# A decoder layer in five stages: what lies ready when a stage begins, and in which order its first work stands

## The reference

```
xz = LN(x) @ W_in; conv of 4 taps, silu, x_dbl = xb @ W_x, dt = softplus(dt_low @ W_dt + b_dt)
h_t = h_(t-1) * exp(A * dt_t) + (x_t * dt_t) * B_t           (1024 channels x 16 states, 224 steps)
y_t = sum over the states of h_t * C_t;   x1 = x + ((y + xb * D) * silu(z)) @ W_out
q = LN(x1) @ Wq + bq (16 heads of 32);  k, v = context @ Wk + bk, context @ Wv + bv
x2 = x1 + softmax(q k^T / sqrt(32)) v @ Wo + bo
router: softmax(gelu(LN(x2) @ rW1 + rb1) @ rW2 + rb2), the two best of 4 experts for each row
out = x2 + sum over both experts e of weight_e * (gelu(LN(x2) @ We1[e] + be1[e]) @ We2[e] + be2[e])
```

## Time and profile before

| | us |
|---|---|
| median of three runs | 2700.24 |
| the profiled execution's own time | 2700.03 |
| its span, from the first to the last recorded instruction | 2698.2 |
| PE busy, share of the span | 2388.7, 89% |
| DVE busy | 1457.8, 54% |
| POOL busy | 1342.5, 50% |
| ACT busy | 1223.0, 45% |

### The profile page before, as it was taken

How to read it: one execution, slowest core, us unless ns; L and a number is a source line. 1 busy time by engine, 2 the same in 40 slices (tenths; PEclk the granted TensorE clock), 3 DMA queues, 4 the chain that set the end, 5 groups by cost and what they waited for, 6 DMA issues and landing times. The chain is left out here.

```text
span 2698.2 us, 39015 instructions
## 1 busy us (share of the span) xinstructions
PE 2388.7 (89%) x14144; PEld 1963.4 (73%) x14144; DVE 1457.8 (54%) x2039; ACT 1223.0 (45%) x2647; POOL 1342.5 (50%) x940
## 2 busy tenths in 40 slices
PE   7999499999999994789999999873989989998994
PEld 6866388888888872457666667652878878888883
DVE  7714599999999972355766676643112121121222
ACT  4345377777777640234444444433333333332331
POOL 2323477777777760266566656634360460009712
PEclk9999699999999996789999999885999999999997
DMA  4327956665666535455554555307130130002303
GB/s 113 131 72 225 273 173 199 203 193 175 194 198 201 161 106 152 125 129 119 132 130 121 140 119 127 94 21 247 47 118 31 48 124 23 16 31 92 118 31 117
DMA packets 236261, 341.90 MB, mean 127 GB/s; under 512 B 34594, under 2 KB 164578, under 8 KB 234962
## 3 DMA queue, kind: packets, MB, share of 16 engines
q1 hardware_dynamic: 213378, 280.03, 36.9%
q0 software_dynamic: 13728, 47.19, 5.6%
q10 hardware_dynamic: 9008, 12.78, 1.4%
HBM read 212.28 MB, written 127.65 MB: 126 GB/s over the span
## 5 line engine op out<-in xcount | busy, mean ns | idle before, releaser
L768 POOL TENSOR_TENSOR s_hc<-s_h,s_Cc 128x896 f32<-128x896 f32 x256 | 495.0, 1938 | 179.2 <-DVE s_h L882 94.9
L882 DVE TENSOR_TENSOR_SCAN s_h<-s_decay,s_ub 128x928 f32<-128x928 f32 x256 | 527.3, 2080 | 13.9 <-PE s_ub L909 7.1
L920 PE MATMUL s_yps<-s_hc,s_ident 128*128 128x224 f32 x2048 | 430.1, 353 | 1.1 <-POOL s_hc L768 1.1
L2000 DVE TENSOR_TENSOR e_hl<-e_ps,e_hh 128x256 fp32r<-128x256 f32 x256 | 108.7, 425 | 574.8 <-ACT e_ps L2040 574.8
L812 ACT ACTIVATE s_decay<-s_dt,s_A 128x224 f32<-128x224 f32 x1024 | 388.0, 470 | 20.2 <-DVE s_h L882 19.1
L920 PEld LDWEIGHTS s_yps<-s_hc,s_ident 128*128 128x128 f32 x2048 | 368.7, 191 | 1.9 <-POOL s_hc L768 1.4
L1219 DVE TENSOR_REDUCE t_nmax<-t_ps 112x1 fp32r<-112x752 f32 x256 | 240.2, 938 | 231.4 <-PE t_ps L1554 230.6
L1175 POOL TENSOR_TENSOR t_part<-t_pT 125x672 f32<-125x672 f32 x128 | 206.7, 1615 | 295.4 <-ACT t_pT L1465 292.5
L2059 PE MATMUL e_ps<-e_xTh,e_w1h 128*128 128x256 f32 x1024 | 292.9, 286 | 45.2 <-DVE e_xTl L1992 45.2
L2039 ACT ACTIVATE e_hh<-e_ps,e_b 128x256 fp32r<-128x256 f32 x256 | 121.6, 475 | 423.4 <-PE e_ps L2061 423.2
L1465 ACT ACTIVATE t_pT<-t_ps 125x448 f32<-125x448 f32 x384 | 181.3, 547 | 261.4 <-PE t_ps L1580 261.0
(11 more groups left out here) (221 smaller groups left out, 4360.9 us busy)
## 6 DMA issues: line engine op xcount, KB each, us to landing
s_ut<-ut_d SPq DMA_DIRECT2D x192, 128.0 KB, 3.3
e_stage<-in_L_ffn_We POOLq DMA_DIRECT2D x24, 1024.0 KB, 5.7
t_k<-kh_d SPq DMA_DIRECT2D x64, 375.0 KB, 6.4
xs_d<-s_zero SPq DMA_DIRECT2D x30, 512.0 KB, 3.5
ut_d<-a_x SPq DMA_DIRECT2D x32, 448.0 KB, 5.5
s_Cc<-cs_d SPq DMA_DIRECT2D x8, 1792.0 KB, 10.1
kh_d<-s_kh SPq DMA_DIRECT2D x32, 375.0 KB, 2.7
kl_d<-s_kl SPq DMA_DIRECT2D x32, 375.0 KB, 3.0
```

The costliest lines, as they stand in the source:

```text
L768: nc.gpsimd.tensor_tensor(hc[:, u % 2, k], h[:, u % 2, k, :, 2:SLOT], Cc[:, b % 2, k], ALU.mult).then_inc(hc_done, 1)
L882: nc.vector.tensor_tensor_scan(h[:, u % 2, k].rearrange("p n t -> p (n t)"), decay[:, u % 2, k].rearrange("p n t -> p (n t)"), ub[:, s % 2 ...
L920: ins = nc.tensor.matmul(yps[:, u % 2, 0:L], ident[:], hc[:, u % 2, :, n], start=(n == 0), stop=(n == NS - 1))
```

## The change

**A region of 36 KB in each partition, `carry`, outlives its stage.** In state_space it holds one of the two buffers of C, of the context and (as `even`, the same bytes in another type) of the matrices of B. In the last batch these are free, and SP loads there what the attention begins with: x and y of batch 0, Wq and W_out (`load_next_stage`, one piece a unit, five in all). In the last batch of scores of the attention (it = 7, sl 1 to 4) W_out, Wq, x and y are no longer needed, and SP loads the experts' first four chunks into the region (`load_first_weights`); in experts it is `stage`. The identity is loaded once for the kernel.

**Last sums.** The last unit's sums are taken by segment: 64 products of 56 columns, 16 as soon as a segment's products are there (`last_sums`), in the place of 16 of 224 columns.

**Attention's first transfers and queries.** Keys of the first two groups and y of batch 1 are loaded ahead of the first queries; the queries of batch 0 are computed in two banks in turn, stored, and loaded again by four heads as soon as they are stored (`load_first_queries`). The rows of the key tile are set by POOL, ahead of its other constants.

**Experts' first splits.** ACT makes the high parts of chunks 0 and 1, then the first tile's split, then chunks 2 to 5; POOL makes those of 6 and 7. DVE makes the low parts of 0 and 1, then the tile's, then 2 and 3, then the gates, then waits for b2.

```diff
@@ state_space, sync
+            def load_next_stage(i):
+                last = B - 1
+                if i == 0:
+                    sp.wait_ge(fill_done, NSEG * CC * last)
+                    sp.wait_ge(v_mm, NC * last)
+                    sp.wait_ge(hc_done, NSEG * CC * last)
+                    sp.dma_start(carry[0:TT, XT_AT:XT_AT + 2 * DM].rearrange("p (u d) -> p u d", u=2),
+                                 x[0].rearrange("(u p) d -> p u d", p=TT)).then_inc(carry_loaded, 16)
...
+                else:
+                    part = slice((i - 3) * 4, (i - 2) * 4)
+                    sp.dma_start(carry[:, WOUT_AT:WOUT_AT + CC * DM].rearrange("p (c n) -> p c n", n=DM)[:, part],
+                                 W_out.rearrange("(c p) n -> p c n", p=P)[:, part]).then_inc(carry_loaded, 16)
...
+                if b == B - 1 and 1 <= c <= 5:
+                    load_next_stage(c - 1)
@@ state_space, tensor
+            def last_sums(u):
+                for k in range(NSEG):
+                    pe.wait_ge(hc_done, NSEG * u + k + 1)
+                    if k == 0:
+                        pe.wait_ge(y_done, u - 1)
+                    for n in range(NS):
+                        ins = nc.tensor.matmul(yps[:, u % 2, k * SEG:(k + 1) * SEG], ident[:], hc[:, u % 2, k, n],
+                                               start=(n == 0), stop=(n == NS - 1))
+                ins.then_inc(sum_done, 1)
...
-            sums(UNITS - 1, range(NS))
+            last_sums(UNITS - 1)
@@ attention
-        wout, wq = sb("wout", [P, CC, DM]), sb("wq", [P, KC, DM])
+        wq = carry[:, 0:KC * DM].rearrange("p (k n) -> p k n", n=DM)
+        gT = carry[:, GT_AT:GT_AT + CC * L].rearrange("p (c t) -> p c t", t=L)
+        wout = carry[:, WOUT_AT:WOUT_AT + CC * DM].rearrange("p (c n) -> p c n", n=DM)
+        xt = carry[0:TT, XT_AT:XT_AT + 2 * DM].rearrange("p (u d) -> p u d", u=2)
...
+        def queries_bank(b, j):
+            return BANK5 if b == 0 and j % 2 == 1 else BANK6
@@ attention, sync
+            def load_first_queries(j):
+                sp.wait_ge(q_stored[j % 2], 32 * (j // 2 + 1))
+                for i, src in enumerate((0, 0, 1)):
+                    sp.dma_start(q3[i * DK:(i + 1) * DK, 0, 4 * j:4 * j + 4].bitcast(F32),
+                                 q_d[src, 0, j].rearrange("(r p) t -> p r t", p=DK)).then_inc(q_first[j], 16)
+            def load_first_weights(n):
+                g, second = n // 2, n % 2
+                if n == 0:
+                    sp.wait_ge(q_mm, KC * B)
+                    sp.wait_ge(out_mm, 2 * B)
+                    sp.wait_ge(x1b_done, 2 * B)
+                    sp.wait_ge(xn_done[0], 2 * B)
...
+                sp.dma_start(carry[:, n * KC * DM:(n + 1) * KC * DM].rearrange("p (k n) -> p k n", n=DM), src).then_inc(w_first[n], 16)
-            sp.dma_start(ident[:], ident_in).then_inc(first_loaded, 16)
-            load_g(0)
-            sp.dma_start(wout[:], rows(W_out)).then_inc(first_loaded, 16)
-            load_x(0)
...
+                if it == -1 and sl == 8:
+                    store_queries(0, 0)
+                    for j in range(KC):
+                        if j + 1 < KC:
+                            store_queries(0, j + 1)
+                        load_first_queries(j)
...
+                if it == B - 1 and 1 <= sl <= 4:
+                    load_first_weights(sl - 1)
@@ attention, gpsimd (and the same taken out of vector)
+            nc.gpsimd.memset(k3[ROWS3:ROWS3 + 2].bitcast(F32), 0.0).then_inc(rows_zeroed, 1)
+            pool.wait_ge(rows_zeroed, 1)
+            pool.wait_ge(w_loaded, 16 * N_W)
+            for r in range(4):
+                nc.gpsimd.tensor_scalar(k3[ROWS3:ROWS3 + 2, :, r], k3[ROWS3:ROWS3 + 2, :, r].bitcast(F32),
+                                        onehot[ROWS3:ROWS3 + 2, r % 2:r % 2 + 1], None, ALU.add).then_inc(rows_set, 1)
@@ attention, tensor
-            pe.wait_ge(first_loaded, 32)
...
-                else:
+                elif b >= 1:
                     pe.wait_ge(q_low, KC * b + j)
+                elif j >= 2:
+                    pe.wait_ge(q_low, j - 1)
@@ experts, gpsimd
-                if n >= 2 * WG:
+                if n >= 2 * WG - 2:
@@ experts, vector
+            for n in range(2):
+                low_weights(n)
...
+                def first(t):
+                    tokens(t)
+                    if e == 0:
+                        for n in range(2, 4):
+                            low_weights(n)
+                        gates()
+                        wait(dve, "b2_loaded", 16)
@@ experts, scalar
-            for n in range(2 * WG):
+            for n in range(2):
+                high_weights(n)
...
+                def first(t):
+                    tokens(t)
+                    if e == 0:
+                        for n in range(2, 2 * WG - 2):
+                            high_weights(n)
+                        wait(act, "b1_loaded", 16)
```

More of the change, by code:

```diff
@@ L910, in fill @@
                                            ut[:, u // 2 % 2, 2 * k + half, u % 2 * P:u % 2 * P + P],
-                                           diag[:, b % 2, 2 * k + half, first:end, 0:width], start=True, stop=True)
+                                           diag[b % 2][:, 2 * k + half, first:end, 0:width], start=True, stop=True)
                 ins.then_inc(fill_done, 1)
@@ new lines, in decoder @@
+        ident = sb("identity", [P, P])
+        mamba_in(nc, a["x"], a[s + "W_in"], a[s + "conv_w"], a[s + "conv_b"], a[s + "W_x"], a[s + "W_dt"], a[s + "b_dt"],
+                 a["identity"], ident, xb_d, z_d, dt_d, ut_d, bt_d, cs_d)
+        with nc.sbuf_tensor("s_even", [P, CARRY], F32R) as even:
+            pass
+        carry = sb("carry", [P, CARRY])
+        state_sems = state_space(nc, a[s + "A_log"], a[s + "D"], a["identity"], ident, even, carry, a["x"], a[s + "W_out"], a[t + "Wq"],
+                                 xb_d, z_d, dt_d, ut_d, bt_d, cs_d, y_d, a["ctxT"], a[t + "Wk"], a[t + "bk"], a[t + "Wv"],
+                                 kh_d, kl_d, v_d, xs_d)
```

225 lines of the change are left out of this document (114 added, 111 removed).

## The result

The changed kernel took 2674.19 us (median of four runs, 2671.8 to 2676.9), the kernel before 2699.67 us beside it: a ratio of 0.9908, 95% interval 0.9891 to 0.9925. Timed again later on another chip it took 2674.27 us, ratio 0.9885 (0.9866 to 0.9904). The forecast was 2673, its range 2657 to 2686. The profiled execution has a span of 2673.5 us, 24.7 less than before.

The account below looks back on a forecast made before the run. PE was taken to be near its limit in every stage, with dips at stage ends. Two shortened dips, at the attention's and experts' starts, gave 2700.0 - 16.3 - 11.0 = 2672.7 us; range 2657 to 2686.

Parts of the forecast that it names:

- Last sums: End of state_space: 128 passes paced by weight loads, 0.106 us each, 13.6 us; 6.2 us lost.
- Attention to the projection: Attention's start: PE waits for no transfer, 1.3 us allowed until it runs; projection keeps its 16.77 us.
- Key rows on POOL: Attention's start: POOL's additions, 4.6 us each, hold DVE's norm; costs 3.7 us (0 to 4.6).
- First queries: Attention, behind the norm: four query groups without waits between, 10.2 us, plus 1.0 for the last split.
- To x: Attention, values' start to landing of x of batch 1: values 14.7 us, then 15.2 us.
- Experts: Experts' start: first product 22.8 us earlier, second layer 13.5 earlier, 2.5 given back by the clock; 11.0 gained.
- E to end: From the experts' first instruction to the kernel's end: 11.0 us less.
- Moved transfers: Loads moved into the last batches of state_space and attention: cost nothing, 0 to 3 us each as bounds.
- X to E: From x of batch 1 landing (DVE's first add of it) to the experts' first instruction: no change forecast.
- Cheap passes: Rival: last unit's sums at 0.05 us a pass, POOL not holding the norm, b2 sooner; 2659 us, chance 0.17.
- late x: Rival: issuing the values takes SP as long as before, x lands at 1102.1; 2684 us, chance 0.19.
- the slower case: Rival: state_space's scan waits for small transfers behind new loads in its last batch; 2716 us, chance 0.03.

Follow-up runs that it names:

- Rows on DVE: Changed kernel with the key rows (a memset and four additions) made by DVE before its first step, not by POOL: 2672.34 us, ratio 0.9880.
- keys and y behind: Changed kernel with keys of the second group and y of batch 1 issued behind the first queries, not ahead: 2678.07 us, ratio 0.9901.
- Gates first: Changed kernel with DVE's six gate operations ahead of its first two low parts, wait for b2 left in place: 2671.31 us, ratio 0.9877.
- b2 at use: Changed kernel with gate operations ahead of the low parts and b2 waited for only where it is added: 2664.56 us, ratio 0.9843.
- region filled late: Changed kernel with the attention's first x, y, Wq and W_out issued behind state_space's whole SP loop, not inside its last batch: 2689.11 us, ratio 0.9941.
- weights in stage: Changed kernel with the experts' first four weight chunks issued by the experts' own SP program, not in the attention's last batch: 2681.44 us, ratio 0.9914.
- changed, again: The changed kernel run once more, nothing edited: 2674.27 us, ratio 0.9885 to the kernel before.
- x before values: Changed kernel with SP issuing x of batch 1 ahead of the values, not behind values, Wo, rows and router weights: 2654.02 us, ratio 0.9802.

## Why the prediction was right, step by step

**Last sums**: right in kind, small in size. Forecast 13.6 us at 0.106 a pass, measured 14.39 at 0.112; start of the stage 6.9 us later relative to POOL's last product, forecast 6.2. The load of 128 columns sets the pace. Scaled from the 31 loads of the earlier trace rows the bound was 0.115; that end was the nearer one.

**Attention to the projection**: PE began 0.04 us behind S (allowed: 1.3) and took 15.65 us instead of 16.77. Both helped, 2.4 us. But 1.1 of it is luck: in the second profile of the same kernel the projection took 16.52, and 15.5 to 16.9 in the others. In the first profile the granted clock was 0.66 in the projection's first 5 us, in the second 0.50.

**Key rows on POOL**: the four additions took 4.14 us each, not 4.6, and held the norm. Ten profiles have the rows on POOL. In six it was the small operation, 3.15 to 3.79 us as forecast (3.7). In four, the first profile among them, it came due before the fourth addition began and slipped in ahead, and the next operation was held instead, 1.8 to 2.1 us. Which of the two it was follows from the projection: due 17.4 to 17.7 us behind S it slipped in, due 18.0 or later it was held. *Rows on DVE* puts the hold at 3 us on the way to the queries' end.

**First queries**: forecast 10.2 + 1.0, measured 9.9 from the first product to the last low part's end. The values began 6.3 us behind that end, not 4.1: the last six loads alone took 4.0 us to issue. The values began at 1058.96 (forecast 1061.0).

**To x**: forecast 29.9 us from there, measured 29.7. It took 41.1 before, so this term holds 11.4 of the 26.0. That it held to 0.2 is partly luck: the values moved at 94 to 99 GB/s, not 104, and took until about 1074.5, 15.5 us for the 14.7; the rest took 14.2 for 15.2. Of the 11.4, *keys and y behind* gives back 5.0. The other 6 no run takes apart. The wait in DVE's third step was there, 23.65 us (forecast: some 20).

**Experts**: first product 9.4 us behind the start (forecast 9.6), second layer 26.4 (forecast 25.6). E to end gave 11.4, forecast 11.0. What the lower clock gives back was put at 2.5 from 5 us at half speed, which no row had shown; measured, the first six products and those behind them took 5.0 us, where they took 2.8 before, so it is 2.2. The last wait was named rightly in one only of the eight profiles with this experts' program, the second of the changed kernel. It should have been b2, with one of the gates' products held. In the first profile b2 was ready 24.2 us behind E, as worked out, yet both products were held, and the gates ended 1.3 us behind it. In the second b2 came last, though again behind two held products. *Gates first* shows b2 next, and *b2 at use* shows what stood behind both.

The prediction said that no row spoke for the second half of the SBUF rule. Its own had one: DVE's product of 64 elements, both inputs in SBUF, took 4.51 us and ended with POOL's low part. The changed kernel has more of them. POOL's low part that began while DVE's fourth low part was still running took 5.27 and 5.30 us, against 4.51 for the next one in the first run; and DVE's product of 64 elements ended with POOL's twice. The Trainium skill, page "SBUF — State Buffer", section "Who interferes with whom", lets a DVE operation with two SBUF inputs and a GpSimd operation that reads SBUF exclude each other, whoever comes first; these rows agree, in both directions. The second product even began 0.5 us before the low part that it waited out; POOL was issuing a transfer then, and what held the product in that half microsecond no run shows.

**Moved transfers**: nothing, as forecast; *region filled late* and *weights in stage* found no cost where they were taken away.

**What the sum did not have**: X to E grew by 5.2 us. PE's idle stretch before X is longer than it was, and its clock behind it would be the first suspect. Stretches behind X, PE's busy time (instructions), granted clock, DMA share, GB/s; before:

```profile
1107.17:1127.17 20.00, 14.04 (x54) 0.76 0.29 71
1127.17:1147.17 20.00, 18.79 (x135) 0.85 0.34 88
1147.17:1167.17 20.00, 13.53 (x103) 0.83 0.79 158
1167.17:1187.17 20.00, 19.15 (x117) 0.83 0.42 101
```

changed:

```profile
1088.70:1108.70 20.00, 15.34 (x49) 0.67 0.16 46
1108.70:1128.70 20.00, 18.43 (x129) 0.81 0.44 108
1128.70:1148.70 20.00, 14.12 (x105) 0.79 0.81 162
1148.70:1168.70 20.00, 18.33 (x109) 0.70 0.43 101
```

changed, again:

```profile
1089.32:1109.32 20.00, 13.69 (x53) 0.76 0.27 70
1109.32:1129.32 20.00, 19.13 (x135) 0.83 0.35 89
1129.32:1149.32 20.00, 13.20 (x97) 0.77 0.79 158
1149.32:1169.32 20.00, 19.15 (x117) 0.81 0.43 101
```

The first profile of the changed kernel reached the next batch's residual 84.1 us behind X, the kernel before 79.7, with PE busy for longer at a lower grant. But the length of the idle stretch does not decide it. PE had stood 22.3 us in the first profile and 24.7 in the second, and the second has nearly the grants of the kernel before and took 81.3. In *rows on DVE* PE had stood 24.1 us, the grants were 0.76 to 0.86, and it took 79.5. Nor does this stretch decide X to E, which was 739.9 in the second profile and 732.5 in *b2 at use*. So my theory of a longer stretch at the lower clock falls, and what divides the executions here is open. From the last residual to E the kernel before took 221.4 us, the thirteen profiles of the others 223.9 and more; with one profile of the kernel before, whether that is the change or chance stays open too. It was not tried apart.

The number is better than the sum behind it. x landed 2.2 us earlier than forecast, though S came 1.3 later; the experts gave 0.4 more; and X to E, which stood at nothing, took 5.2. That makes 2.6 too little in the profiled execution and 1.5 in the median, and that it is no more is luck. Cheap passes, late x and the slower case all fell: no 0.05 us pass, x issued 24.7 us behind the values, no wait for a transfer in the scan's last batch.

## What to carry to other kernels

At a stage's end, find the one transfer for which the pipeline stops, and move that one first: one transfer put ahead of the values gave nearly as much by the median (20 us, from runs 20 us apart) as the change as a whole (25). When work is cut finer to start sooner, count the weight loads: passes of 56 columns took 0.113 us each here, the pace of their loads, and not a quarter of 0.197. And look at what a small operation meets on the other engine: 64 elements a partition cost 5 us beside POOL and 0.23 before POOL had work.

## What the runs showed of the hardware that was not expected

- One small transfer, rb2, held SP for 6.2 to 10.3 us in every profile, where the two behind it needed 0.3 to 0.6. It always stood behind the loads of Wo and the router's weights, but it also spreads four numbers over 128 partitions; which of the two makes it dear no run separates. The 2.0 MB queued ahead in *keys and y behind* delayed x by 5.0 us besides their issue.
- A shorter idle stretch of PE gave more than its length in the experts: 7.9 us from the move and 2.1 from the clock, 0.50 against 1.00 behind the wait.
- In the attention it gave less: with S to X 24.9 to 27.4 us shorter, *x before values* gained 20 in the median and 6 to 9 in the one profile, whose granted clock in the 80 us behind X was 0.70 to 0.88.
- Which operation of DVE's norm POOL's addition held, and whether for 2 us or for 3 to 4, hung on 0.3 us of timing (due 17.7 or 18.0 us behind S).
